# A rounding chain between the feed-forward product and the second LayerNorm of a transformer layer

## What is computed

```python
def _L0_ffn_ref(x, weight, bias):
    x_mat = quantize_e4m3(x2d, SCALE).astype(jnp.float16)
    w_mat = quantize_e4m3(weight, SCALE).astype(jnp.float16)
    out2d = (x_mat @ w_mat.T).astype(jnp.float32) * (SCALE * SCALE)
    out2d = out2d + bias
    return out2d.reshape(B, N, -1)

x = _layernorm(x + attention(x))   # projections with bias, rotary embedding, softmax
x = _layernorm(x + _L0_ffn_ref(x, L0_ffn_weight, L0_ffn_bias))
```

## Time and profile before

| what | us |
|---|---|
| time of three runs | 1210.85, 1210.77, 1192.70 (median 1210.77) |
| the profiled execution, its time | 1192.03 |
| the profiled execution, its span on the slowest core | 1190.5 |
| the spans of the eight cores | 1182.5 to 1190.5 |
| VectorE busy | 504.9 (42%) |
| ScalarE busy | 700.8 (59%) |
| TensorE (matmuls) busy | 842.1 (71%) |

### The profile page before, as it was taken

The page is one execution under the profiler, slowest core; times in us unless marked ns, Lnnn a source line. Parts: engine busy times, 40 slices in busy tenths (PEclk is TensorE's granted clock), DMA queues, the critical chain, the costliest instruction groups (busy, mean ns, idle before and its releaser), DMA issues.

```text
span 1190.5 us, 11688 instructions; the slowest of 8 cores (1182.5 to 1190.5 us)
## 1 busy us (share of the span) xinstructions
PE 842.1 (71%) x3648; PEld 312.6 (26%) x3648; DVE 504.9 (42%) x951; ACT 700.8 (59%) x745; POOL 130.0 (11%) x69
## 2 busy tenths in 40 slices
PE   1287675849887878777778877787877754666766
PEld 1243222314322222222222222222222221222222
DVE  5128776883202132222222222222222237878876
ACT  0000000000188888888898888888888867666653
POOL 0007755770000000000000000000000000000000
PEclk9998877879999999999998999999999995777777
DMA  8671135111160000000000000000000000010012
GB/s 118 95 126 36 36 61 115 36 36 36 61 239 1 1 1 18 0 19 0 18 1 1 18 1 18 1 18 1 1 18 0 1 19 1 18 53 36 36 54 89
DMA packets 15179, 42.80 MB, mean 36 GB/s; under 512 B 2192, under 2 KB 2320, under 8 KB 15120
## 3 DMA queue, kind: packets, MB, share of 16 engines
q0 software_dynamic: 6672, 15.73, 7.4%
q1 hardware_dynamic: 8448, 26.33, 7.3%
HBM read 36.81 MB, written 8.39 MB: 38 GB/s over the span
## 4 chain that ended last, share of the span: by engine, by line
PE 32%; ACT 29%; issue 10%; DMA 9%; POOL 9%; DVE 8%; SPq 3%; ACTq 0%; DVEq 0%; POOLq 0%
ACT PT L445 23%; PE ps L460 15%; PE ps_sc L432 10%; PE ps L291 4%; DMA xb<-x 4%; POOL rs L256 3%; POOL rs L254 3%; POOL ro L257 3%; PE ps L728 2%; DMA wb<-wqT 1%; SPq L269 1%; DMA qT<-ro 1%; DMA wb<-wkT 1%; DVE zf L742 1%; ACT dump_t L753 1%
## 5 line engine op out<-in xcount | busy, mean ns | idle before, releaser
L445 ACT ACTIVATE PT<-ps_sc,k_s 128x1024 bf16<-128x1024 f32 x512 | 545.0, 1111 | 84.1 <-PE ps L460 78.4
L460 PE MATMUL ps<-PT,va 128*65 128x512 bf16 x1024 | 329.0, 404 | 0.8 <-ACT PT L445 0.8
L432 PE MATMUL ps_sc<-qT,kT 64*128 64x512 bf16 x1024 | 206.6, 392 | 143.4 <-ACT PT L445 135.2
L445 ACT ACT_TABLE_LOAD x1 | 1.3, 1283 | 319.9 <-PE ps_sc L432 319.9
L227 PE MATMUL ps<-xT,wb 128*128 128x512 bf16 x512 | 127.4, 416 | 46.4 <-DVE qraw L238 45.4
L432 PEld LDWEIGHTS ps_sc<-qT,kT 64*128 64x128 bf16 x1024 | 62.8, 93 | 335.7 <-issue 335.7
L499 DVE RECIPROCAL rc_sb<-ps 128x1 f32<-128x1 f32 x256 | 20.2, 151 | 276.3 <-PE ps L485 276.2
L728 PE MATMUL ps<-wfq,yqT 128*128 128x512 bf16 x256 | 89.1, 525 | 60.1 <-DVE qsc L690 26.0
L460 PEld LDWEIGHTS ps<-PT,va 128*65 128x65 bf16 x1024 | 73.1, 111 | 122.7 <-issue 122.7
L475 DVE COPY oa_sb<-ps 65x1024 f32<-65x1024 f32 x32 | 39.1, 1221 | 149.1 <-PE ps L460 149.1
L227 PEld LDWEIGHTS ps<-xT,wb 128*128 128x128 bf16 x512 | 53.3, 105 | 120.2 <-issue 70.4
(11 more groups left out here) (77 smaller groups left out, 638.1 us busy)
## 6 DMA issues: line engine op xcount, KB each, us to landing
xf<-x SPq DMA_DIRECT2D x1, 8192.0 KB, 31.1
out<-xf SPq DMA_DIRECT2D x16, 512.0 KB, 2.6
xb<-x POOLq DMA_DIRECT2D x4, 1024.0 KB, 10.4
qT<-ro SPq DMA_DIRECT2D x32, 128.0 KB, 2.4
kT<-ro SPq DMA_DIRECT2D x32, 128.0 KB, 2.4
wfs<-wfT POOLq DMA_DIRECT2D x8, 512.0 KB, 3.5
wb<-wqT POOLq DMA_DIRECT2D x1, 2048.0 KB, 17.6
wb<-wkT POOLq DMA_DIRECT2D x1, 2048.0 KB, 15.2
```

The costliest lines, as they stand in the source:

```text
L432: return e.matmul(ps_sc[:, slot, half * 512:(half + 1) * 512], kT[r0:r0 + 64, hp, kt * 128:(kt + 1) * 128], qT[r0:r0 + 64, hp, q0:q0 + 512 ...
L445: return e.activation(PT[:, slot, :], ps_sc[:, slot, :], AF.Exp, bias=consts[:, C_SHIFT:C_SHIFT + 1], scale=0.125)
L460: return e.matmul(ps1[0:65, base:base + 512], va[:, kt, h * 65: h * 65 + 65], PT[:, slot, half * 512:(half + 1) * 512], start=(kt == 0), s ...
```

## The change

In stage 6 the product in PSUM goes through a chain like that of the stages 2 to 4 before `yf` is added. The scale is 2^24 in place of 512, the constant is C + 74 in place of C + 67 (a new column 2 of `cder`, `t_C74`), and the scratch `qs16` is new (3 x 1024 float32 a partition; one for all tiles, guarded by `rot_use["r16"]`). `z2` then takes its input from `qs16` and scales it back. The whole chain (Abs and Ln on ScalarE, two instructions on VectorE, Exp on ScalarE, four on VectorE) is issued within stage 6, between the matmuls of the tile and stage 5.

```diff
+    t_C74 = A("V", lambda e: e.tensor_scalar_add(cder[:, 2:3], cder[:, 0:1], 74.0),
+              waits=[t_C67])
...
+    qs16, _qs16_cm = sb("qs16", (128, 3, 1024))
...
-            tk["z2"] = A("V", lambda e, zs=zs, ys=ys, poff=poff: e.tensor_add(
-                zf[:, zs, :], ps1[:, poff:poff + 1024], yf[:, ys, :]),
-                waits=[last, rot_use["zf"].get(zs)])
+            r16w = [rot_use["r16"]]
+            rA = A("S", lambda e, poff=poff: e.activation(
+                qs16[:, 0, :], ps1[:, poff:poff + 1024], AF.Abs,
+                bias=0.0, scale=2.0 ** 24), waits=[last] + r16w)
+            rL = A("S", lambda e: e.activation(
+                qs16[:, 1, :], qs16[:, 0, :], AF.Ln,
+                bias=consts[:, C_025:C_025 + 1], scale=1.0), waits=[rA, t_k])
+            rM = A("V", lambda e: e.tensor_scalar(
+                qs16[:, 0, :], qs16[:, 1, :], consts[:, C_ILN2:C_ILN2 + 1],
+                63.5, ALU.mult, ALU.add), waits=[rL, t_k])
+            rE = A("V", lambda e: e.tensor_scalar(
+                qs16[:, 1, :], qs16[:, 0, :], cder[:, 0:1], cder[:, 2:3],
+                ALU.add, ALU.subtract), waits=[rM, t_C74])
+            rS = A("S", lambda e: e.activation(
+                qs16[:, 0, :], qs16[:, 1, :], AF.Exp, bias=0.0,
+                scale=consts[:, C_LN2:C_LN2 + 1]), waits=[rE])
+            rMt = A("V", lambda e: e.tensor_scalar(
+                qs16[:, 1, :], qs16[:, 0, :], 1.0, cder[:, 0:1],
+                ALU.max, ALU.mult), waits=[rS])
+            rP = A("V", lambda e, poff=poff: e.scalar_tensor_tensor(
+                qs16[:, 0, :], ps1[:, poff:poff + 1024], 2.0 ** 24,
+                qs16[:, 1, :], ALU.mult, ALU.add), waits=[rMt])
+            rQ = A("V", lambda e: e.tensor_sub(
+                qs16[:, 2, :], qs16[:, 0, :], qs16[:, 1, :]), waits=[rP])
+            rot_use["r16"] = rQ
+            tk["z2"] = A("V", lambda e, zs=zs, ys=ys: e.scalar_tensor_tensor(
+                zf[:, zs, :], qs16[:, 2, :], 2.0 ** -24, yf[:, ys, :],
+                ALU.mult, ALU.add), waits=[rQ, rot_use["zf"].get(zs)])
```

## The result

| | kernel before | changed kernel |
|---|---|---|
| median of all runs, us | 1195.76 | 1340.32 |
| ratio of the times, 95% interval | | 1.1218 (1.1203 to 1.1234) |
| profiled execution, its time, us | 1192.03 | 1335.94 |
| its span on the slowest core, us | 1190.5 | 1334.4 |

The change makes the kernel 12% slower. Between the two profiled executions the difference is 143.9 us, where the working gave 147.2. Over all runs each kernel's times fall into two levels (1191 to 1200 and 1203 to 1215 us before, 1336 to 1342 and 1354 to 1360 changed), and the ratio above is taken between the lower ones.

What follows compares the result with a forecast made beforehand. VectorE and ScalarE handing work to each other were taken as the pace, not TensorE. The terms 8.94 + 115.0 + 9.15 + 9.31 + 4.78 = 147.2 us on the profiled 1192.03 gave 1339 us, range 1329 to 1364.

Steps and rivals of the forecast that it cites:

- The length of the chain: Stage 6, Abs to z2: eight start-to-start steps summed from the old trace, nearly end to end, 8.94 us.
- The two terms with no row: Abs and P reading PSUM: taken as 1.06 and 1.23 us, bounded at 0.1 us either way and at most 0.1 more.
- The place of Abs: Steady rounds: Abs starts where tqe did, 0.64 us after the old z2; +9.58 us, round 22.2 instead of 12.60.
- The first tile: First of 16 tiles: ScalarE idle when its matmuls end, Abs starts where z2 did; +8.94 us.
- Tiles 2 to 13: Twelve steady tiles, each delayed by Abs's later start plus the chain: 12 x 9.58 = +115.0 us.
- Tiles 14 and 15: Near the end: old z2 waits for matmuls, 0.43 and 0.27 us, vanish; +9.15 and +9.31 us.
- The last: Last tile: matmuls on the path, z2 distance 13.92 us instead of 9.14; +4.78 us.
- No cost ahead of the stage, no table load: Kernel start: t_C74 taken as nothing, else 0.3 us. Rival of ScalarE table reloads: 41 us more, 1380, chance 1%.
- Clock: TensorE may drop to 1.2 GHz; only the last matmuls count, 8.37 for 7.21 us: +1.2, 1340; counted in main case.
- the cover: Steady rounds: matmuls end 15.0 us after Abs, next Abs due at 22.2; 7 us to spare even at their slowest.
- The waits that I named: Idle stretches in the new round: VectorE before M 3.1 us, ScalarE before Exp 1.9, VectorE before Mt 1.3.
- Overlap: Rival: added work fills idle stretches, only VectorE's surplus counts, 4.0 x 16 = 64 us, 1256 us; chance 3%.

Runs made afterwards that it cites:

- the kernel with the closed loop: Kernel before with the product rounded by one float16 copy in ScalarE's idle time and yf's chain replaced by an 8-bit copy and VectorE copy; ratio 0.9741.
- the one with the loop opened: Against the 8-bit-copy kernel: next tile's transposes and tqe issued ahead of the matmuls, float16 copy and z2 one round later; 1138.87 us, ratio 0.9558 to the kernel before.

## Why the prediction was right

It was right in its number (1339 against 1340.3) and in its steps; the distances from one `z2` to the next show each of them. That the two numbers agree to about a microsecond is partly chance: 1339 was put on the level of the profiled execution, and this one took 1335.9. The ends of the range are a little off what its own terms give: 1339 less 5 and 3 is 1331, not 1329, and 18 us more at the top gives 1365, not 1364.

- *The length of the chain*, 8.94 us: 8.89. The two terms with no row came out in the lower half of their bounds: Abs from PSUM takes 1.01 us in place of 1.06, and 1.10 in place of 1.15 to the start of Ln; P from PSUM takes 1.23 us, what `z2` took from there. As predicted, the larger fixed cost of PSUM reads that the Trainium skill gives ("VectorE: DVE Perf Modes", "The TRN2 errata") does not show: the trace of the changed kernel has 1.23 us for P with PSUM as well as for Q without.
- *The place of Abs*, 0.64 us behind the old `z2`, and the round, 22.2 us: 22.13 or 22.14 in each of the first ten distances. This step carried the sum, and the experiments bear it out from three sides: halves of the chain cost their halves, moving one unrelated instruction ahead of it costs that instruction, and the same work in other places costs 70 us in place of 145.
- *The first tile*, +8.94: 8.90. *Tiles 2 to 13*, 12 x 9.58 = 115.0: from the distances 113.8. Here the term was a little too large: most tiles gained 9.53 to 9.55, and tiles 2 and 4, whose old distances were 12.94 and 12.88 and not 12.60, gained 9.20 and 9.26. (The old trace has such rounds of 12.9 in these two places; the new one has none.)
- *Tiles 14 and 15*, +9.15 and +9.31: 9.04 and 9.22. *The last*, +4.78: 13.84 - 9.14 = 4.70, with the matmuls on the path as said.
- The sum over these is 145.7 us in place of 147.2; the rest of the difference to 143.9 lies ahead of the stage: the first tile's matmuls ended 1.75 us earlier than in the trace before, and 1.6 us of this is there already when the profiled core's attention ends.
- *No cost ahead of the stage, no table load*: there is one load of 1283 ns in the trace after, as before. *Clock*: the granted clock of the stretch fell from 0.76 to 0.63, and it cost nothing in the steady rounds, where 16 matmuls took up to 6.55 us and the cover held; the last tile's matmuls took 5.38 + 1.9 us, not the 8.37 of the low end. TensorE was busy 123.08 of 320.31 us, so idle over half of the stage, as said.
- The waits that I named came out at 2.94, 1.87 and 1.35 us against 3.1, 1.9 and 1.3.
- *Overlap*, the rival with 3%: the experiments show that it belongs to another order of the queues, and that even there its size was too low: the rival filled VectorE's gap first, and the gap stays. With the chain spread, the measured ratio is 1.0594 (some 70 us, where it had 64).

What stays open is why rounds of 12.9 us occur now and then among those of 12.6 in the kernel before; no run was made for it, and it is 0.3 us each. The trace shows only where the time goes, and it is not one place: VectorE is idle 0.30 us right before `z2` at 1020.26, ScalarE 0.37 us before the `Exp` of L654 at 1042.98. Six of the eight experiments have one to three such rounds as well.

## What to carry to other kernels

Where two engines hand work to each other in in-order queues, as here, and neither has ready work ahead of the waits, an added chain costs its whole length from start to start, crossings included, if all of it is issued at one place: read the place of the first instruction and the steps from a timeline where the same chain once ran bare, add them up, and ignore the busy shares. The same work cost half here when the VectorE parts that wait on ScalarE were issued later, behind work that is ready, and a short operation on ScalarE cost nothing when it was issued where that engine's bracket shows idle time and its reader after it. Before spreading a chain of arithmetic that rounds, see whether a write to a narrower type does the rounding in one instruction, and compare the values. And when a round gets shorter, don't multiply the gain by the number of tiles: the last rounds of a pipeline may already be short, and a new loop can hold them back.

## What the runs showed of the hardware

- A ScalarE copy from PSUM into a float16 tile takes 1.02 us for 128x1024, as long as Abs from there into float32 (1.01); a ScalarE copy to 8-bit floats 1.06 us; VectorE's cast from 8-bit floats to bf16 0.69 us.
- The 16 matmuls of a tile, each of 512 columns, take between 3.61 and 6.55 us. In the kernel before, one set took 3.61 us (0.23 us each) at a granted clock of 1.00 throughout, which is the upper level, 2.4 GHz; in the kernel with the closed loop a set took 6.51 us (0.41 us each) at a mean granted clock of 0.55, so nearly all of it at the lower level, 1.2 GHz. In the kernel with the closed loop TensorE was busy 123.54 of 140 us (88%) at a granted clock of 0.67; in the one with the loop opened it was busy 81.20 of 100 us at 0.80, and the mean length of one of these matmuls fell from 595 to 458 ns:

```profile
1000.00:1140.00 140.00, 123.54 (x385) 45.68 (x384) 83.14 (x157) 78.07 (x141) 0.00 (x0) 0.67 0.12 49
```

```profile
L703 PE MATMUL ps<-wfq,yqT 128*128 128x512 bf16 x256 | 103.9, 595 | 22.3 <-ACT yqT L692 22.3
```

```profile
1010.00:1110.00 100.00, 81.20 (x303) 34.22 (x304) 65.89 (x126) 62.26 (x115) 0.00 (x0) 0.80 0.15 58
```

```profile
L703 PE MATMUL ps<-wfq,yqT 128*128 128x512 bf16 x256 | 74.8, 458 | 0.2 <-ACT yqT L692 0.2
```

The first two are the stretch and the group of matmuls of the kernel with the loop closed, the other two of the one with it open. What made the clock come out higher was not isolated. A high busy share of TensorE was in part slow matmuls.
